# Recomputing three batches of hidden sums in place of five, in groups of nine

## The reference, cut to what matters

```python
def _L0_xattn_ref(q, k, v):          # q = layernorm(x), k = v = ctx
    r = 0.9 * r + (k * v)            # along the batches' tokens
    return q * r
x = x + _L0_xattn_ref(_layernorm(x), ctx, ctx)

def quant_act_uint8(x):
    s = max(max(x), 1e-8) / 255      # one maximum over ALL elements
    return clip(round(x / s), 0, 255) * s
def quant_linear(x, w, b):           # w: int8 with a scale per row
    return einsum('btd,fd->btf', quant_act_uint8(x), quant_w(w)) + quant_b(b)
h = relu(quant_linear(layernorm(x), w1, b1))
x = x + quant_linear(h, w2, b2)
```

## Time and profile before

| | |
|---|---|
| median of the runs | 1365.98 us |
| profiled execution, its own time | 1367.56 us |
| span in the profile | 1365.7 us |
| PE busy | 1296.0 us, 95% |
| DVE busy | 970.6 us, 71% |
| ACT busy | 902.8 us, 66% |
| moved by DMA | 418.33 MB, mean 306 GB/s |
| second product (L944), first and last | from 838.84 us to 1359.82 us |

### The profile page before, as it was taken

How to read it: one execution, slowest core, us unless ns; L and a number is a source line. 1 busy time by engine, 2 the same in 40 slices (tenths; PEclk the granted TensorE clock), 3 DMA queues, 4 the chain that set the end, 5 groups by cost and what they waited for, 6 DMA issues and landing times.

```text
span 1365.7 us, 17623 instructions
## 1 busy us (share of the span) xinstructions
PE 1296.0 (95%) x5706; PEld 594.9 (44%) x5706; DVE 970.6 (71%) x1396; ACT 902.8 (66%) x1283; POOL 291.0 (21%) x777
## 2 busy tenths in 40 slices
PE   6778999998699999999999998999999999999998
PEld 3343443343344444444444443444444444444443
DVE  5989999999577777777777775665556456556555
ACT  5687787787675757757667566777476575674770
POOL 2969999999200000000000000000000000000000
PEclk9989999999799999999999999999999999999999
DMA  9887999995696979969879655899899898898832
GB/s 356 323 330 264 331 336 350 335 339 204 231 364 241 346 267 336 349 238 362 316 268 366 231 214 219 337 404 402 290 364 378 290 377 341 319 375 322 316 131 93
DMA packets 124610, 418.33 MB, mean 306 GB/s; under 512 B 9572, under 2 KB 9592, under 8 KB 111992
## 3 DMA queue, kind: packets, MB, share of 16 engines
q1 hardware_dynamic: 75192, 249.59, 47.2%
q10 hardware_dynamic: 49344, 167.79, 35.6%
HBM read 245.38 MB, written 171.97 MB: 306 GB/s over the span
## 4 chain that ended last, share of the span: by engine, by line
PE 66%; POOL 16%; DVE 8%; issue 7%; ACT 2%; POOLq 1%; DMA 1%; DVEq 0%; ACTq 0%
PE ps L887 37%; PE ps L944 24%; DVE work L790 2%; PE ps L912 2%; DVE work L804 2%; POOL rstd L448 2%; POOL pw L432 2%; PE ps L866 1%; POOL pw L434 1%; POOL pw L431 1%; DVE work L799 1%; POOL rstd L466 1%; POOL pw L429 1%; POOL pw L428 1%; POOL zrow L446 1%
## 5 line engine op out<-in xcount | busy, mean ns | idle before, releaser
L887 PE MATMUL ps<-xq,w1T 128*128 128x512 f16 x2368 | 531.1, 380 | 1.4 <-DVE xq L748 1.4
L620 ACT ACTIVATE xq<-xq,hb,hs 128x512 f16<-128x512 f32 x432 | 321.4, 805 | 180.3 <-PE ps L944 171.7
L944 PE MATMUL ps<-w2T,xq 128*128 128x512 f16 x1888 | 427.9, 381 | 6.3 <-ACT xq L620 2.0
L887 PEld LDWEIGHTS ps<-xq,w1T 128*128 128x128 f16 x2368 | 230.9, 98 | 275.3 <-issue 3.0
L739 DVE TENSOR_REDUCE work<-xq 128x2 f32<-128x1024 f32 x216 | 263.5, 1220 | 113.4 <-ACT xq L566 113.4
L566 ACT ACTIVATE xq<-ps 128x1024 f32<-128x1024 f32 x216 | 221.2, 1024 | 151.0 <-PE ps L887 150.8
L866 PE MATMUL ps<-xq,work 128*128 128x512 f32 x640 | 290.1, 611 | 32.2 <-ACT xq L499 21.6
L944 PEld LDWEIGHTS ps<-w2T,xq 128*128 128x128 f16 x1888 | 183.6, 98 | 237.3 <-DVE work L790 12.2
L866 PEld LDWEIGHTS ps<-xq,work 128*128 128x128 f32 x640 | 122.6, 195 | 197.4 <-issue 146.8
L499 ACT ACTIVATE xq<-ps,rstd 128x512 f32<-128x512 f32 x128 | 78.0, 689 | 62.5 <-POOL rstd L466 56.1
L790 DVE TENSOR_TENSOR work<-ps,cs_bc 128x512 f32<-128x512 f32 x128 | 86.2, 688 | 41.2 <-PE ps L944 34.4
(11 more groups left out here) (107 smaller groups left out, 696.8 us busy)
## 6 DMA issues: line engine op xcount, KB each, us to landing
hidden_scratch<-xq SPq DMA_DIRECT2D x200, 512.0 KB, 5.9
xq<-hidden_scratch ACTq DMA_DIRECT2D x200, 512.0 KB, 6.7
work<-x_scratch SPq DMA_DIRECT2D x33, 1024.0 KB, 7.0
xq<-in_x_dram SPq DMA_DIRECT2D x32, 1024.0 KB, 7.8
x_scratch<-xq SPq DMA_DIRECT2D x32, 1024.0 KB, 5.8
xq<-in_ctx_dram ACTq DMA_DIRECT2D x31, 1024.0 KB, 5.4
out_dram<-work SPq DMA_DIRECT2D x31, 1024.0 KB, 9.9
work<-x_scratch ACTq DMA_DIRECT2D x29, 1024.0 KB, 6.7
```

Source lines behind the costliest of these rows:

```text
L620: act.activation(hq[c % HQ], src[:, c % 2, :], ACT.Relu, bias=hb[:, q:q + 1], scale=hs[:, q:q + 1]).then_inc(h_scaled, 1)
L887: last = pe.matmul(bank, w1T[:, k, f * P:(f + 1) * P], xq_rows(b, k), start=(k == 0), stop=(k == KD - 1))
L944: last = pe.matmul(acc_bank(i), src[:, i * P:(i + 1) * P], w2T[:, q, :], start=first, stop=final)
```

## The change

Three batches are recomputed where there were five, and 27 are stored where there were 25. The groups of stage three become nine stored batches and a recomputed one (three times), where they were five and one (five times). The fresh chunks of a group spread over nine turns: 1, 1, 1, 1, 1, 1, 2, 2, 2 in the first group and 1, 1, 2, 2, 2, 2, 2, 2, 2 in the others, where they were 2, 2, 2, 3, 3 and then 3, 3, 3, 3, 4.

```diff
-RECOMPUTED = (3, 9, 15, 21, 27)
+RECOMPUTED = (5, 15, 25)
...
-FRESH_AT = {2: (6, 9), 3: (5, 8, 11), 4: (5, 7, 9, 11)}
+FRESH_AT = {1: (7,), 2: (6, 9)}
```

## The result

The changed kernel takes 1333.87 us (median of 4 runs, 1333.36 to 1334.86) against 1365.72 us for the kernel before beside it. The ratio is 0.9767, 95% interval 0.9750 to 0.9784. The forecast was 1333, range 1331 to 1342.

The account below looks back on a forecast made before the run. PE was taken to bound stages two and three. Removed matmuls (-27.6) and DVE's late L790 (-5.3) sum to -32.9 us, other terms 0, taking the median from 1365.98 to 1333.1, forecast 1333, range 1331 to 1342.

Parts of the forecast that it names:

- Fresh matmuls: Stage three: two batches fewer recomputed take 128 matmuls off PE, saving 27.6 us.
- DVE's late L790: Stage three: turns with three fresh chunks vanish, and with them 18 waits of 0.295 us, saving 5.3 us.
- forecast margin of 1 us in turns of one: Stage three, turns with one fresh chunk: DVE is ready 1 us before PE gives up its first bank.
- ACT, 0: Stage three: ACT's 32 more L620 fit in 2.7 us spare in the shortest new turn with loads, cost 0.
- Stage two, 0: Stage two: nine stored batches in a row still take 14.71 us each, cost 0, at most 4 us.
- slack that I put at 4.9 us: Stage two: time left between a store's landing plus ACT's copy and the batch of 14.71 us.
- Transfers in stage three, 0: Stage three: shorter turns ask for up to 429 GB/s, two buffers take the lag, cost 0, at most 8.6 us.
- up to 5 us more lag on SP's chain: First group of stage three: at 405 GB/s six turns of one in a row add 5.2 us of transfer lag.
- A: Stage three: only the matmuls go, DVE's late L790 brings nothing, 1338.4 us; 10% together with the long store stretch.
- B: Stage three: turns with one fresh chunk are paced by the transfers, 8.6 us more, 1341.7 us; chance 9%.
- C: Stage three: SP's wait for its output store paces every stored turn, slower at 1399 us; chance 3%.
- The median: Whole kernel: the profiled run lay 1.6 us above the median of 1365.98, so the median becomes 1333.1 us.

Follow-up runs that it names:

- experiment 1: Kernel before, with fresh chunks of a turn of three behind middle chunks 5, 7, 9 instead of 5, 8, 11: 1360.94 us, ratio 0.9959.
- experiment 3: Changed kernel with recomputed batches side by side (13, 14, 15) instead of (5, 15, 25): 1332.60 us, ratio 0.9747 to the kernel before.

## Why the prediction was right, step by step

*Fresh matmuls, 27.6 us.* Right. L887 has 128 fewer, and 32.9 less the 5.2 of experiment 1 leaves 27.7.

*DVE's late L790, 5.3 us.* Right in size and in place: 5.2 us in experiment 1. The forecast margin of 1 us in turns of one is 1.10 in the trace.

*ACT, 0.* Right: ACT is busy 96.38 of 120 us in the first window above, and PE's matmuls wait for it once, 2.0 us at the start of stage three, as before.

*Stage two, 0.* Right: 14.71 us a batch, and experiment 3 shows it holds for 14 in a row. (The slack that I put at 4.9 us is 14.71 - 8.9 - 1.02 = 4.8.) Share 0.99 at 356 GB/s was not a full machine; the landings told the truth that the share did not.

*Transfers in stage three, 0.* Right in cost, but by a smaller margin than I gave. I let the transfers hold 405 GB/s, the rate asked for; their ceiling is 415 GB/s, and two windows of 20 us before the change show 414 and 415, which I did not trust. I expected up to 5 us more lag on SP's chain in the first group. Its store landings grew from 12.4 to 16.0 us, 3.6, and passed the length of a turn. From then on SP's wait held back seven stores in a row. The last output before the worst of them, and SP's timeline:

```profile
995.03 1.28 DVE L804 TENSOR_TENSOR work<-work 128x512 f32<-128x512 f32 x2
```

```profile
983.73 0.43 SPq L380 DMA_DIRECT2D out_dram<-work  x1
999.59 0.33 SPq L376 DMA_DIRECT2D work<-x_scratch  x1
999.97 0.43 SPq L380 DMA_DIRECT2D out_dram<-work  x1
```

The output was ready at 995.03 + 1.28 = 996.31 us and its store went out at 999.97, 3.7 us late, when the store of 983.73 had landed. I had also counted the bias of a slot as due two turns later at the place that it has in a turn of one. The recomputed turn has no fresh chunks, and DVE adds the bias at its start. The `x2` load of 999.59 us lands 7.8 us later, at 1007.4, and its L799 starts at 1011.77: 4.4 us are left, where the least in the kernel before is 14.7. So the 0 held by 4.4 us. What I had not seen is that a store landing longer than a turn delays every store behind it, by an amount that adds up. It did not matter with three recomputed batches and decided with two.

*Rivals.* A is refuted by experiment 1. B's transfers are full in the turns of one, 415 GB/s, and PE is unmoved by it; a pace set by the total shows with one recomputed batch and GpSimd's queue. C's price did not come near: it needed transfers below 383 GB/s, and full windows show 415. But its mechanism, SP's wait for its output store, is at work in the first group already, and with two recomputed batches it costs PE time. The Trainium skill's page SBUF — State Buffer, in its summary of rules, would have 358 GB/s; full windows here show 415. Its HBM Reference page, in the section on specifications, says that a core streaming alone measures about 425 GB/s, and with this the trace nearly agrees.

*The median.* It fell by 31.85 us and not 32.9. The profiled execution before lay 1.6 us above its median, the one after at it; what remains beside stage three's 32.93 us is about 1 us, no more than the single runs of one kernel differ by (1.1 and 1.5 us here). That the time came within 1 us of 1333 is in part luck.

## What to carry to other kernels

Divide the time of a repeated unit by the matmuls in it: what is over is a wait, and here 0.295 us times 18 was a sixth of the gain and could be had alone with one number. When work is traded for bytes, count bytes per unit against a rate that a window has really carried, then ask of every buffered chain separately how long its transfers take to land and when they are due; the chain with the least slack decides, not the mean. Where an engine waits for a transfer to land before it issues the next, that landing is the shortest turn it allows, in whatever order the issues stand. A spare engine's queue is worth trying there, while the total is full too.

## What the runs showed of the hardware

The 16 DMA engines carried loads and stores together at 411 to 417 GB/s and no more, in every window of 100 us and longer with a share of 1.03, in nine kernels. A share of 0.99 to 1.00 went with 356 to 401 GB/s.

Queues do not divide the full engines evenly. With two recomputed batches ACT's, with an estimated six or seven loads of 512 KB in flight (12 us to land at this rate), got 284 GB/s, SP's, with one or two transfers of 1 MB, 130. An output store of 1 MB with no other transfer on its queue still took 14.0 us to land, beside ACT's and GpSimd's; at the end of the changed kernel, when ACT loads nothing, it took 4.3. Whether the number in flight or the form of the transfers sets the division was not tried.

An issue of a load on ACT took 0.33 us in most cases, but up to 5.26 us with one recomputed batch and GpSimd's queue, where loads took 20.8 us to land in the median, and ACT's activations stood behind it.
